# Two heads in one block of 32 columns of the value product, the small stack in six transfers, and a new order of a batch's jobs

## The reference

```python
att = q k^T / sqrt(8)             # 16 heads of 8, causal
S = relu(att[:, 0]); S[..., 0] = 0; S = S * (1 - eye)     # from head 0 alone
FF = cumsum(S shifted down by one query, axis=queries)
att = att - FF[:, None]
# each query keeps the keys with the smallest FF (102 - 1 of them) and itself
y = softmax(where(keep, att, -inf)) @ v
attention = y @ w_proj.T + b_proj
# ffn: 8 experts that share wi and wo, each with a LoRA of rank 16; top 2 by a softmax gate
out = sum_e gate_e * (relu(x wi^T + bi + (x A_e^T) B_e^T) wo^T + bo)
```

## Time and profile before

| | |
|---|---|
| median of 3 runs | 660.26 us (660.19 to 662.8) |
| the profiled execution | 663.88 us, span 661.9 us |
| PE, PEld busy | 561.8 us (85%), 382.5 us |
| DVE, ACT, POOL busy | 505.3 us (76%), 378.0 us (57%), 445.7 us (67%) |
| mean granted clock of PE | 0.958 |

### The profile page before, as it was taken

One profiled execution on the slowest core, in us unless ns is written; L12 is line 12 of the kernel. 1 busy time (PEld: TensorE's weight loads), 2 busy tenths in 40 slices (PEclk: granted clock), 3 DMA queues, 4 the chain that ended last, 5 costly groups with the idle time before them and its releaser, 6 DMA issues.

```text
span 661.9 us, 16486 instructions
## 1 busy us (share of the span) xinstructions
PE 561.8 (85%) x5434; PEld 382.5 (58%) x5434; DVE 505.3 (76%) x1832; ACT 378.0 (57%) x815; POOL 445.7 (67%) x756
## 2 busy tenths in 40 slices
PE   4636879989888899889998898989998899899994
PEld 1413555766466665656566565666566565776583
DVE  7679798667997679857897769867897769975351
ACT  3452776565765565754756566664756556455542
POOL 7506948696578746796478955798478956496451
PEclk9656999999999899989999999999999999999998
DMA  4152052134001520025100430025000430000000
GB/s 100 25 63 27 1 63 35 30 47 61 1 17 28 65 30 1 18 47 63 11 18 17 60 45 1 17 43 70 9 1 18 60 44 1 2 14 5 1 2 17
DMA packets 30068, 19.56 MB, mean 30 GB/s; under 512 B 6089, under 2 KB 29856, under 8 KB 29984
## 3 DMA queue, kind: packets, MB, share of 16 engines
q1 hardware_dynamic: 29984, 18.50, 19.5%
HBM read 3.22 MB, written 2.10 MB: 8 GB/s over the span
## 4 chain that ended last, share of the span: by engine, by line
PE 41%; DVE 19%; POOL 15%; issue 11%; ACT 7%; SPq 4%; DMA 1%; DVEq 1%; ACTq 0%; POOLq 0%
PE ps_t L923 10%; POOL ar L549 9%; PE ps_o L942 9%; PE ps_s L910 6%; PE ps_m L855 4%; SPq L407 4%; DVE ar L1330 4%; ACT work L648 2%; PE ps_m L851 2%; DVE work L1150 2%; PE ps_m L867 2%; ACT pr L734 2%; POOL hsum L563 1%; PE ps_m L873 1%; PE ps_m L885 1%
## 5 line engine op out<-in xcount | busy, mean ns | idle before, releaser
L549 POOL TENSOR_SCALAR ar<-ar,mx 128x512 f32<-128x512 f32 (+3 forms) x512 | 280.2, 561 | 171.4 <-DVE mx L1330 165.1
L734 ACT ACTIVATE pr<-ps_t 128x512 f32<-128x512 f32 (+1 forms) x352 | 192.4, 558 | 80.9 <-PE ps_t L923 78.8
L1330 DVE CUSTOM_DVE_ANT_0 ar<-ps_s,mask 128x256 f32<-128x256 f32 (+2 forms) x384 | 202.9, 550 | 33.2 <-PE ps_s L910 32.3
L923 PE MATMUL ps_t<-ident,ar 128*128 128x128 f32 x1280 | 202.6, 277 | 16.5 <-POOL ar L549 11.0
L923 PEld LDWEIGHTS ps_t<-ident,ar 128*128 128x128 f32 x1280 | 156.2, 142 | 57.2 <-POOL ar L549 27.4
L910 PE MATMUL ps_s<-ks,qs 96*128 96x512 bf16 (+3 forms) x512 | 130.4, 307 | 11.7 <-DVE mx L1327 6.0
L942 PE MATMUL ps_o<-pr,va 128*32 128x128 f32 x2560 | 98.8, 282 | 7.6 <-ACT pr L734 6.1
L942 PEld LDWEIGHTS ps_o<-pr,va 128*32 128x32 f32 x2560 | 63.4, 111 | 48.5 <-ACT pr L734 31.2
L910 PEld LDWEIGHTS ps_s<-ks,qs 96*128 96x128 bf16 x512 | 43.1, 99 | 56.5 <-issue 27.1
L719 ACT ACTIVATE h<-ps_m,bi_col 128x512 f32<-128x512 f32 x64 | 43.9, 687 | 54.9 <-PE ps_m L855 54.2
L855 PE MATMUL ps_m<-zm,b_t 128*128 128x512 f32 x128 | 67.7, 610 | 8.7 <-ACT h L719 8.7
(11 more groups left out here) (227 smaller groups left out, 772.1 us busy)
## 6 DMA issues: line engine op xcount, KB each, us to landing
qs<-parts SPq DMA_DIRECT2D x42, 128.0 KB
ks<-parts SPq DMA_DIRECT2D x42, 128.0 KB
xs<-in_L_attn_x SPq DMA_DIRECT2D x8, 256.0 KB, 3.0
out<-res SPq DMA_DIRECT2D x8, 192.0 KB, 2.0
first_heads<-parts SPq DMA_DIRECT2D x72, 8.0 KB
qs<-parts SPq DMA_DIRECT2D x12, 64.0 KB
ks<-parts SPq DMA_DIRECT2D x12, 64.0 KB
out<-res SPq DMA_DIRECT2D x8, 64.0 KB, 10.5
```

Source lines behind the costliest of these rows:

```text
L549: nc.gpsimd.tensor_scalar(col, col, -1.0, mx[:, t % NA_RING, j:j + 1], ALU.mult, ALU.add)\
L734: nc.scalar.activation(pr[:, u % NP_RING, 0:w], ps_t[u % NT_RING][:, 0:w], ACT.Exp, scale=-1.0)\
L923: last = nc.tensor.transpose(ps_t[u % NT_RING][:, P * j:P * j + P], ar[:, u % NA_RING, P * j:P * j + P], ident[:, :])
L1330: nc.vector.tensor_tensor_reduce(out=ar[:, t % NA_RING, w * j:w * j + w], in0=ps_s[t % NS_RING][:, w * j:w * j + w], in1=mask[:, k % 2, OF ...
```

## The change

- **Value product.** Two heads share a block of 32 partitions of ps_o. va holds pairs of heads, 41 columns apart: eight values and a one, seven columns of no use, nine zeros, seven of no use, then the second head's values and its one. The window of 32 columns for the first head starts at the pair, that for the second 16 columns later, so each puts zeros where the other's nine results lie, and both accumulate in one place. Heads are taken in `ORDER`. A tile then needs 256 columns, and two tiles fit the bank: one copy to out_t, one ot and one yt job for two tiles. Each job of ot still has four transposes, each of yt has two. The number of matrix products of `weigh` is the same.
- **v copies.** ACT copies each chunk of v in two parts (even and odd heads): four small copies in a v job and not one.
- **proj** is cut in tiles 0 and 1 and tiles 2 and 3; bias_rows shrinks to two blocks.
- **Small stack.** Each transfer carries the parts of q and of k (six in place of twelve), and SP issues them ahead of the store of proj0.
- **s0** has no storage of its own: it lies in rows 0, 1, 2 of `work` and at the end of row 1. ACT waits for the mask of the batch before, and not for its scan.
- **The steps of all jobs** are new.

```diff
-OW = 512 // NH
+OW = 32
+HALF_OW = OW // 2
+PAIR = 41
+OUT_COLS = HALF_OW * NH
+ORDER = [8 * (i // 8) + 2 * (i % 4) + i % 8 // 4 for i in range(NH)]
-FIRST_FFN = ffn_jobs(6, (17, 19), (22, 24, 27, 30), (34, 36))
-FFN_JOBS = ffn_jobs(4, (8, 8), (15, 18, 21, 23), (29, 31))
-OT_AT, YT_AT, PROJ_AT = (12, 19, 36, 50), (17, 22, 39, 52), (40, 55)
+FIRST_FFN = ffn_jobs(6, (17, 18), (19, 22, 24, 30), (40, 42))
+FFN_JOBS = ffn_jobs(4, (5, 13), (16, 18, 22, 24), (30, 31))
+OT_AT, YT_AT, PROJ_AT = (20, 50), (21, 51), (46, 54)
 FIRST_AT = {
...
-    "flag": 24, "mask_0": 24, "mask_1": 24, "v0": 21, "v1": 26, "marks_middle": 26, "top0_middle": 26,
-    "replace0_middle": 27, "top1_middle": 27, "replace1_middle": 28, "marks_wide": 25, "top0_wide": 25,
-    "replace0_wide": 26, "top1_wide": 26, "replace1_wide": 27, "last": 29, "mask_2": 30, "mask_3": 32,
-    "route": 30, "choices": 37, "share": 38,
+    "flag": 24, "mask_0": 24, "mask_1": 24, "v0": 10, "v1": 18, "marks_middle": 27, "top0_middle": 27,
+    "replace0_middle": 28, "top1_middle": 30, "replace1_middle": 31, "marks_wide": 25, "top0_wide": 25,
+    "replace0_wide": 26, "top1_wide": 28, "replace1_wide": 29, "last": 31, "mask_2": 32, "mask_3": 32,
+    "route": 26, "choices": 38, "share": 39,
 }
 SECOND_AT = {
-    "moments": -23, "root": -23, "norm": -5, "xt": -4, "q": 9, "k": 10, "rest_q": 10, "second_q": 11,
-    "third_q": 12, "rest_k": 11, "second_k": 12, "third_k": 12,
+    "moments": -23, "root": -23, "norm": -5, "xt": -4, "q": 7, "k": 12, "rest_q": 8, "second_q": 9,
+    "third_q": 10, "rest_k": 13, "second_k": 14, "third_k": 15,
 }
 PREP_AT = {
-    "moments": -22, "root": -17, "norm": -15, "xt": -12, "q": -11, "k": -10, "rest_q": -10, "second_q": -9,
-    "third_q": -8, "rest_k": -9, "second_k": -8, "third_k": -7, "v0": 11, "v1": 13, "route": 14, "choices": 22,
-    "share": 23, "s0": 3, "s1": 5, "s2": 7, "s3": 9, "scan0": 6, "scan1": 6, "scan2": 10, "scan3": 12, "f0": 9,
-    "f1": 12, "f2": 13, "f3": 15, "search": 16, "under": 22, "reach": 23, "marks_narrow": 24,
-    "marks_middle": 26, "marks_wide": 27, "top0_narrow": 24, "top0_middle": 26, "top0_wide": 29,
-    "replace0_narrow": 27, "replace0_middle": 28, "replace0_wide": 30, "top1_narrow": 34, "top1_middle": 31,
-    "top1_wide": 35, "replace1_narrow": 35, "replace1_middle": 31, "replace1_wide": 35, "flag": 37,
-    "mask_0": 38, "mask_1": 38, "mask_2": 41, "mask_3": 45,
+    "moments": -27, "root": -17, "norm": -15, "xt": -12, "q": -11, "k": -10, "rest_q": -10, "second_q": -9,
+    "third_q": -8, "rest_k": -9, "second_k": -8, "third_k": -7, "v0": 15, "v1": 15, "route": 15, "choices": 21,
+    "share": 29, "s0": 3, "s1": 5, "s2": 7, "s3": 8, "scan0": 6, "scan1": 9, "scan2": 10, "scan3": 11,
+    "f0": 11, "f1": 11, "f2": 14, "f3": 14, "search": 15, "under": 22, "reach": 23, "marks_narrow": 28,
+    "marks_middle": 24, "marks_wide": 26, "top0_narrow": 28, "top0_middle": 25, "top0_wide": 27,
+    "replace0_narrow": 28, "replace0_middle": 26, "replace0_wide": 29, "top1_narrow": 31, "top1_middle": 36,
+    "top1_wide": 29, "replace1_narrow": 35, "replace1_middle": 36, "replace1_wide": 35, "flag": 40,
+    "mask_0": 40, "mask_1": 40, "mask_2": 44, "mask_3": 47,
 }
...
+        s0_place = ((0, 0), (1, 0), (2, 0), (1, 3 * P))
+        def s0(j, lo, hi):
+            row, at = s0_place[j]
+            return work[:, row, at + lo:at + hi]
...
                         wait_full(sp, "s3", m - 1)
-                        for t in range(2):
-                            sp.wait_ge(split, 2 * m + t + 1)
-                            part = (Q_PART, K_PART)[t]
-                            for j in range(len(part)):
-                                sp.dma_start(first_heads[8 * j:8 * j + 8, t, :], parts[0:P:NH, t, part[j], :])\
-                                    .then_inc(topped, 16)
+                        sp.wait_ge(split, 2 * m + 2)
+                        for j in range(len(Q_PART)):
+                            lo, hi = Q_PART[j], 3 + K_PART[j]
+                            sp.dma_start(first_heads[8 * j:8 * j + 8, :, :],
+                                         parts[0:P:NH, :, :, :].rearrange("p t j c -> p (t j) c")[:, lo:hi + 1:hi - lo, :])\
+                                .then_inc(topped, 16)
...
-                        store(sp, k, 0)
                         if k + 2 < B:
                             make_first_heads(k + 2)
+                        store(sp, k, 0)
...
-                                    act.wait_ge(scanned, NA * (n - 1) + j + 1)
+                                    act.wait_ge(mask_done, NA * (n - 1) + s0_place[j][0] + 1)
...
-                                copy(va[:, into(n), both, 0:NH * VW].rearrange("p a (h d) -> p a h d", d=VW)[:, :, :, 0:HD],
-                                     m3[:, :, 0:P].rearrange("p a (h d) -> p a h d", d=HD), name, n, False)
+                                for i, a in enumerate(half):
+                                    for s in range(2):
+                                        copy(va[:, into(n), a, 0:NH // 2 * PAIR]
+                                             .rearrange("p (h d) -> p h d", d=PAIR)[:, :, OW * s:OW * s + HD],
+                                             m3[:, i, 0:P].rearrange("p (h s d) -> p h s d", s=2, d=HD)[:, :, s, :],
+                                             name, n, False)
...
-                            for a in range(NA):
+                            for a in (1, 3):
                                 if t == NU * kk + LAST[a] + LAG_P + OUT_LAG:
                                     act.wait_ge(summed, NG * kk + GROUPS * (a + 1))
...
+                        block, odd = divmod(group, 2)
+                        col = OUT_COLS * (a % 2) + P * block
                         for c in range(a + 1):
                             for j in range(QUAD):
...
-                                last = nc.tensor.matmul(ps_o[OW * j:OW * j + OW, P * group:P * group + P],
-                                                        va[:, k % 2, c, VW * hh:VW * hh + OW],
+                                from_v = PAIR * (ORDER[hh] // 2) + HALF_OW * odd
+                                last = nc.tensor.matmul(ps_o[OW * j:OW * j + OW, col:col + P],
+                                                        va[:, k % 2, c, from_v:from_v + OW],
                                                         pr[:, (NU * k + unit) % NP_RING, at:at + P],
-                                                        start=(c == 0), stop=(c == a))
+                                                        start=(c == 0 and odd == 0), stop=(c == a and odd == 1))
...
-                                o3 = m[:, :].rearrange("p (h d) -> p h d", d=OW)
+                                o4 = m[:, :].rearrange("p (g d) -> p g d", d=HALF_OW)
...
                                 nc.vector.tensor_tensor(
-                                    y[:, a, :, :], o3[:, :, 0:HD],
-                                    rec[:, :].rearrange("p (h o) -> p h o", o=1).to_broadcast([P, NH, HD]), ALU.mult)\
+                                    y[:, 2 * a:2 * a + 2, :, :].rearrange("p a h d -> p (a h) d"), o4[:, :, 0:HD],
+                                    rec[:, :].rearrange("p (g o) -> p g o", o=1).to_broadcast([P, 2 * NH, HD]), ALU.mult)\
                                     .then_inc(dve_read, 1)
```

More of the change, by code:

```diff
@@ L370, in store @@
                     wait_read(sp, ("proj0", "proj1")[part], k)
-                    lo, hi = ((0, NA - 1), (NA - 1, NA))[part]
+                    lo, hi = ((0, 2), (2, NA))[part]
                     sp.dma_start(out_d[bass.ds(k, 1), :, lo:hi, :].rearrange("o p a c -> p (o a) c"),
@@ L477, in _ @@
                     link(nc.gpsimd.memset(va[:, :, :, :], 1.0))
+                    for p in range(NH // 2):
+                        link(nc.gpsimd.memset(va[:, :, :, PAIR * p + HALF_OW:PAIR * p + HALF_OW + VW], 0.0))
                     nc.gpsimd.memset(half_mark[:, :], -MARK / 2).then_inc(const, 1)
@@ L518, in pool_prepares @@
                                 wait_read(pool, f"s{a}", n)
-                                edge = s0[:, FOFF[a]:FOFF[a] + P]
+                                edge = s0(a, 0, P)
                                 nc.gpsimd.affine_select(out=edge, in_=edge, compare_op=ALU.is_gt, fill=0.0, base=0,
@@ L722, in _ @@
                                 a = int(name[2])
-                                if n >= 1 and a in (0, 3):
-                                    wait_full(act, ("proj0", "proj1")[a == 3], n - 1)
-                                copy(yt[:, a, :], m[:, 0:P], name, n)
+                                if n >= 1:
+                                    wait_full(act, f"proj{a}", n - 1)
+                                copy(yt[:, 2 * a:2 * a + 2, :].rearrange("p a t -> p (a t)"), m[:, 0:2 * P], name, n)
                         u = t - LAG_T
@@ L870, in fill @@
                             a = int(name[2])
-                            pe.wait_ge(taken, NA * n + a + 1)
```

(19 more changed lines are left out.)

41 lines of the change are left out of this document (20 added, 21 removed).

## The result

The changed kernel takes 628.85 us, the median of four runs (626.7 to 635.17), against 660.23 for four of the kernel before on the same chip: a ratio of 0.9539, interval 0.9484 to 0.9594. That is 31.4 us saved where 10.7 were forecast; 628.85 lies 20.8 us under the forecast and 7 under the range. The profiled execution took 626.7 us (span 625.0), against 663.88 (661.9), so these two traces differ by 37. Ratios and intervals leave out a run that took over 1.5% more than the fastest of its kernel.

What follows compares the result with a forecast made beforehand. POOL was taken as full in a pass's first 22 us, DVE in its last 34, PE near-full; -4.0 - 4.2 - 3.0 - 3.5 + 2.1 + 1.2 + 0.7 = -10.7 gave 653.2, as median 649.6; range 636 to 666.

Steps and rivals of the forecast that it cites:

- rival 2: Everything opens: clock never falls, all transposes count, half of both waits and 1.0 us a DVE-stretch pass gained; 635, chance 0.21.
- Masks later: mask_0 to mask_3 move to later steps, among those where POOL has most; +0.2 us a pass, +1.2 in all.
- The two zm products: They go from step 8 together to 5 and 13; their 5.4 us wait lies under POOL's bound, 0, -5.4 at most.
- Transposes: Sets of four out_t transposes on PE fall from 32 to 16; nine of 0.44 us counted, -4.0, bounds 0 to -7.0.
- y, yt and moments: In DVE's full stretch, one y job leaves and moments moves from step 22 to 17; 0.7 us a pass, -4.2.
- DVE under 93%: Sign expected in the trace after: DVE busy under 93% in the last 34 us of a pass.
- Small stack: Six transfers ahead of proj0's store: PE's wait on them goes, POOL is late next; 0.5 us a pass, -3.0.
- Clock: Falls to half clock in passes' first 22 us, behind PE's waits: two of three go, -3.5, bounds 0 to -5.1.
- v copies: On ACT, four copies of 64 elements replace one of 256, at 0.22 us each; +0.3 a pass, +2.1 in all.
- Rival 3: ACT takes over between steps 15 and 20, PE waiting on its va or h copies; slower, 669, chance 0.20.
- Tail: At the end of the run the last set is for two tiles, so its y, yt, proj and res take longer: +0.7.
- Rival 1: Full engines hold: POOL paces a pass's first stretch, DVE's round trips the last; only the last pass gains; 660, chance 0.15.

## Why the prediction was wrong

The sign, the kinds of instruction and most small terms were right; the mechanism that brought the gain was priced with the wrong sign, and the result lies nearest to rival 2 (635), without its reason.

*The step that failed* is the price of the new tables. The forecast had them at +1.2 ("Masks later"), at 0 for "The two zm products" and for proj0, in part of the -4.2 for DVE, and with no term for the scans and the other moves. With pairing and small stack in place they are worth 39.5 us as a whole. The forecast said "The sum of work is the same, only two steps of shifts leave the full part". It was the place that counted: put back alone, the flag and masks cost 7.7 us, and the zm products 4.0, not resolved from 0. The misreading behind it is one of windows. I had read POOL 97% full from the start of a pass, and the windows that I called the last 34 us of a pass stop 7 to 10 us short of its end. The steps 36 to 44, which gave 17.9 us of the gain (71.3 to 53.4), lay mostly in neither, and two thirds of the gain lie between step 36 and step 4.

*Transposes*, -4.0: should have been 0. They were done twice without loss. PE was near full, but it waited on POOL in the one stretch, and in the other (94% now) the time was there too.

*y, yt and moments*, -4.2: the product takes 0.424 us, where 0.43 was estimated, but the reciprocal, also twice as wide, takes 0.352, where 0.255 was left in the sum: 1.55 us a pass, not 1.4. The premise, DVE 93% full in the last 34 us, was read from the windows above; over the true ones it was 89%, so the sign "DVE under 93%" could not have failed. Moments and the selection together gave 2.5, not resolved from 0. The term was too big, if anything.

*Small stack*, -3.0: mis-sized and not additive. Alone it costs 11 in the median, 5.3 of it in the six passes of its trace; with zm apart the two gain 3.6; in the new order the number of issues is worth 4.4, not resolved from 0, but the place ahead of the store 34. That "the wait goes" was right, and so was that POOL "is late next". What was missed is that PE's wait for zm then grows, from at most 1.2 to 1.8 us, with the clock's fall behind it.

*Clock*, -3.5: before there are four pieces of 3.4 us at 0.50 after the first pass (one more than the earlier trace rows cover, in the last 34 us of pass 6), after there are two. A piece costs (1 - 0.92) x 22 = 1.8 us, so 3.5 gained: right in size, in these two traces.

*v copies*, +2.1: the small copy takes 0.263 us, over the 0.22 taken; a kernel with one copy gained 2.2, not resolved from 0. Rival 3 did not come: steps 15 to 18 take 5.88 us for 5.58, and no wait of PE on va or h grew (7.5 us on h, 8.7 before).

*Value product* 0: 97.8 us against 98.8 for the same 2560 instructions. *Tail* +0.7: the last pass took 0.6 more. *First pass* 0, within 3: 2.1 shorter, starting 1.3 later. *s0 in work* 0: not tried alone.

*Rival 1* (only the last pass gains) is refuted, though its 97% was real: POOL's share rose to 99%, and the pass still grew shorter. A full engine in one window does not say that the windows around it can't shrink, nor that its own work can't be spread.

*What stays open.* The four pieces put back one by one in the kernel after cost 7.7 + 4.0 + 4.4 + 2.5 = 18.6 of 31.4 us, and only the 7.7 is clear of the runs' spread. Added to the kernel before, three of them together gained nothing that can be told from no change. So they work only within the rest of the new order, and which of the other moves (proj0 and ot, the scans, f, share) opens it was not separated. proj0 put back at step 40 was not tried.

## What to carry to other kernels

Cut the windows at the program's own steps and across the end of a loop, and look for the engine that is idle *between* its jobs there: a long job or a round trip on another engine, put among the jobs of the one that sets the pace, can leave it without input (here for 0.6 to 1.5 us each time). Name the cause of a gap only from what the other engine did before it ended. Ask of each edit how much it takes from the pacing engine in its stretch; in a stretch that another engine paces, seven microseconds of matrix work came and went for nothing. A wait that goes moves on: try it together with what is late next, since alone it cost 11 us and with the next pair spread that loss was gone.

## What the runs showed of the hardware

A smaller sum of PE's waits did not keep the clock up. With the small stack alone, the 10.4 and 5.4 us of waits on the transfer and on zm became 10.6 on zm, and after the first pass the clock fell five times and not four. Nor does the length of one idle piece decide it. PE's longest idle piece in steps 4 to 12 is 1.76 us there, in each of passes 1 to 6, and the clock fell in five of them. In the kernel after it is 1.65 to 1.75 us in passes 2 to 6, and the clock fell in two; with the transposes doubled it is 1.26 to 1.33 us, and no window after the first pass was below 1.00 (PE busy 145.31 of 154 us in the first stretches, for 142.90). But in pass 6 of the kernel before it fell behind a piece of 0.89. What decides it is not shown. The Trainium skill, page "TensorE: Matmul & The Clock Gate", section "What's actually happening", says that the throttled state is the default and activity releases it. The doubled transposes, with no piece at 0.50 after the first pass where after has two, agree with that; that they save time is not resolved (625.32 against 628.85).

POOL's instruction depends on what DVE does. In the kernel before, the same edge of 128x128 takes 1.28 us beside DVE's scan and 0.29 four microseconds later, beside DVE's zm product. Passes 1, 5 and 6 show the same 1.28 to 1.29 beside a scan:

```profile
373.88 1.28 POOL L520 TENSOR_SCALAR_AFFINE_SELECT s<-s 128x128 f32<-128x128 f32 x1
...
377.68 0.29 POOL L520 TENSOR_SCALAR_AFFINE_SELECT s<-s 128x128 f32<-128x128 f32 x1
```

```profile
373.44 2.71 DVE L1091 TENSOR_TENSOR_SCAN ft<-ones,s 128x511 f32<-128x511 f32 x2
```

The Trainium skill, page "SBUF — State Buffer", section "Who interferes with whom", says that DVE and GpSimd share one pair of ports under an exclusive lock. The trace agrees in that the edge takes four times as long beside a scan; that the ports are the reason was not tested.
